# Query/key pieces moved and awaited by token span, and a new order of the side steps in a fused convolution, attention and expert kernel

## The reference, cut to what matters

```
x = x + conv(group_norm(x))      # 16 images, 192 channels, 32 x 32
t = tokens(x)                    # 1024 tokens of 192 channels per image
t = t + attention(layer_norm(t)) # 6 heads of 32, window of 33 keys around each token, plus token 0
t = t + experts(layer_norm(t))   # 4 experts (hidden 768), each token goes to the best 2

conv:  a linear recurrence with 16 states over rows and over columns, both directions,
       plus a gate g = sigmoid(W2 gelu(W1 layer_norm(x))),  result g*y + (1-g)*x
```

## Time and profile before

| | us |
|---|---|
| median of 3 runs | 3558.24 |
| lowest, highest | 3534.18, 3563.71 |
| the profiled execution's own time | 3556.88 |
| its span, first to last instruction | 3555.1 |
| PE busy | 2775.2 (78% of the span) |
| DVE busy | 1944.4 (55%) |
| ACT busy | 1040.5 (29%) |
| POOL busy | 916.0 (26%) |
| granted PE clock, mean | 0.754 of full |

### The profile page before, as it was taken

How to read it: one execution, slowest core, us unless ns; L and a number is a source line. 1 busy time by engine, 2 the same in 40 slices (tenths; PEclk the granted TensorE clock), 3 DMA queues, 4 the chain that set the end, 5 groups by cost and what they waited for, 6 DMA issues and landing times. The chain is left out here.

```text
span 3555.1 us, 51690 instructions
## 1 busy us (share of the span) xinstructions
PE 2775.2 (78%) x18529; PEld 2241.9 (63%) x18529; DVE 1944.4 (55%) x5684; ACT 1040.5 (29%) x2533; POOL 916.0 (26%) x672
## 2 busy tenths in 40 slices
PE   0467686878887888878888787888878788878877
PEld 0356575667666766667666666766666676667545
DVE  4544454555655555555555555565555556555645
ACT  0031413232332424242331423232142323314222
POOL 0001212050503314050411405041230505023344
PEclk9756676786868687786868778686867869676989
DMA  4330304151332515141242514134151514324375
GB/s 44 110 97 13 82 18 114 32 138 20 94 88 59 119 55 128 32 123 35 76 101 55 128 32 129 29 84 97 50 128 32 137 21 100 82 56 112 87 173 118
DMA packets 300095, 286.96 MB, mean 81 GB/s; under 512 B 218204, under 2 KB 259390, under 8 KB 289216
## 3 DMA queue, kind: packets, MB, share of 16 engines
q1 hardware_dynamic: 239104, 192.25, 20.7%
q0 software_dynamic: 50880, 52.59, 8.5%
q10 hardware_dynamic: 9856, 38.80, 3.6%
HBM read 133.73 MB, written 73.59 MB: 58 GB/s over the span
## 5 line engine op out<-in xcount | busy, mean ns | idle before, releaser
L1562 PE MATMUL PSUM<-XT,WB 128*128 128x512 f16 x2010 | 568.9, 419 | 26.4 <-DMA META<-slots 26.3
L834 ACT ACTIVATE HF<-PSUM,WB 128x512 f32<-128x512 f32 x402 | 275.6, 689 | 825.1 <-PE PSUM L1562 821.0
L857 ACT ACTIVATE PSPT<-PSUM,NMX 94x126 f32<-94x126 f32 x1056 | 286.1, 361 | 726.9 <-DVE NMX L1148 492.8
L1634 PE MATMUL PSUM<-VW,PSPT 126*94 126x33 f32 x2112 | 374.3, 350 | 62.1 <-DVE PSPT L1132 54.8
L1634 PEld LDWEIGHTS PSUM<-VW,PSPT 126*94 126x94 f32 x2112 | 350.6, 279 | 112.7 <-DVE PSPT L1132 112.7
L1580 PE MATMUL PSUM<-WB,HHI 128*128 128x192 f16 x1608 | 411.6, 256 | 0.2
L1094 DVE TENSOR_SCALAR HHI<-HF 128x512 f16<-128x512 f32 x402 | 175.1, 436 | 431.8 <-ACT HF L834 426.3
L1581 PE MATMUL PSUM<-WB,HHI 128*128 128x192 f16 x1608 | 410.7, 255 | 0.0
L1582 PE MATMUL PSUM<-WB,HLO 128*128 128x192 f16 x1608 | 409.9, 255 | 0.0
L728 POOL DMA_INDIRECT out_dram<-Y,META x228 | 362.5, 1590 | 147.0 <-issue 77.3
L1562 PEld LDWEIGHTS PSUM<-XT,WB 128*128 128x128 f16 x2010 | 210.6, 109 | 218.1 <-issue 65.4
(11 more groups left out here) (275 smaller groups left out, 4861.7 us busy)
## 6 DMA issues: line engine op xcount, KB each, us to landing
WB<-weights SPq DMA_DIRECT2D x67, 1600.0 KB, 7.5
QST<-QT SPq DMA_DIRECT2D x288, 64.6 KB
KST<-X SPq DMA_DIRECT2D x144, 86.6 KB
KST<-XN SPq DMA_DIRECT2D x144, 86.6 KB
XR<-in_x ACTq DMA_DIRECT2D x16, 768.0 KB, 7.1
out_dram<-X ACTq DMA_DIRECT2D x32, 384.0 KB, 3.2
weights<-WB ACTq DMA_DIRECT2D x4, 1600.0 KB, 7.0
GUP<-TGU SPq DMA_DIRECT2D x256, 8.0 KB, 1.8
```

The lines of the kernel that those rows point to most:

```text
L834: act.activation(HF[:, k % 2, :], PSUM[:, 4 + k % 2, :], ACT.Gelu, scale=1 / (X_UP * W_UP), bias=bias).then_inc(f["gelu_done"], 1)
L857: e = act.activation(PS[0:QS, n % 2, h, :], PSUM[0:QS, n % 2, h * KS:(h + 1) * KS], ACT.Exp, bias=NMX[:, b, n % 2, h:h + 1])
L1562: mm = pe.matmul(dst, WB[:, ws, w:w + 128], XT[:, xs, chunk, :], start=(n == 0), stop=(n == 4))
L1634: mm = pe.matmul(PSUM[0:QS, 2, O_COL + c:O_COL + c + VC], PT[:, n % 2, h, :], VW[:, b, c:c + VC], start=True, stop=True)
```

## The change

1. **Pieces by span.** Piece n is now of kind (query, key) n // 2 % 2, half n % 2 and span n // 4: four pieces (both halves of query and of key) finish a span. The extra query column of token 0 goes with span 0.
2. **Moves by span.** `qk_moves` waits per span for four split pieces and issues 36 copies for that span, 108 in all, each over the span's 3 or 4 blocks; each span has a semaphore of its own. PE's `attention` waits for span 0 ahead of block 0, for span 1 ahead of block 4 and for span 2 ahead of block 8.
3. **Steps by number.** `til(count, k)` yields until step k. PE: the states are projected at step 3, ahead of the output product (4) and not behind it; the recurrence (L1444) at 10 and not 12; the gate products at 15, 16, 18, 19; `turn_tokens(i, 1)` at 13 and not 9, router at 16 and not 12; the output product of `rest` at 12 and not 15, `turn_tokens(i, 0)` at 20 and not 22, router at 23 and not 25; the mixing at 27 to 34 and not 26 to 34; the transposes of the first norm at 37 and 39 and not 41 and 42; the pieces from 45 and not 47. DVE: both gated inputs at 4 and not at 5 and 6, ahead of `add_attention`; `norm_tokens` at 8 and 15, not 6 and 18; `gates` at 26, positions 38, schedule 39 (before: 27, 35, 36).
4. **First norm in halves.** Statistics, power, shift, ACT's normalization (`first_norm`) and DVE's split (`first_halves`) run for tiles 0 to 3 while tiles 4 to 7 are mixed.
5. **Orders.** `block_out(j-1)` comes behind `split` of chunk 1 of block j, ahead of that iteration's side steps, and not at chunk 2 behind them. SP: `state_moves(i+1)` ahead of `expert(i, 2)`, the last copy (`state_place`) behind it. POOL: `token_rstd(i, 0)` ahead of `conv_states(i+1)`. Banks: output product 0 to 3, router 2, prefix sums 3, with the waits that follow from it.

```diff
+        def til(count, k):
+
+            while count[0] < k:
+                count[0] += 1
+                yield
...
+        GATE_AT, MIX_AT = (15, 16, 18, 19), 27
...
+        def piece_of(n):
+
+            return n // 2 % 2, n % 2, n // 4
...
-        ROUTE_BANK = [1, 2]
+        ROUTE_BANK = [2, 2]
         X2_FREE = ["x2a_free", "x2b_free"]
-        WO_BANK = [3, 2, 2, 3]
+        WO_BANK = [0, 1, 2, 3]
...
+
+            def state_place(i):
                 sp.wait_ge(s["hs_permuted"], at("hs_permuted", i, 1))
                 sp.dma_start(XG[97:113, 0, :], HST2).then_inc(s["hs_placed"], 16)
 
             def qk_moves(i):
-                for to, halves, rows in ((QST, [QHL[:, :, 0], QHL[:, :, 1]], (0, 0, 1)), (KST, KHL, (0, 1, 0))):
-                    for oh in range(2):
-                        sp.wait_ge(s["qk_split"], at("qk_split", i, 3 * oh + (3 if to is QST else 9)))
-                        for h in range(HH):
+                for span, (b0, b1) in enumerate(SPANS):
+                    sp.wait_ge(s["qk_split"], at("qk_split", i, 4 * (span + 1)))
+                    moved = s[f"qk_moved{span}"]
+                    for to, halves, rows in ((QST, [QHL[:, :, 0], QHL[:, :, 1]], (0, 0, 1)), (KST, KHL, (0, 1, 0))):
+                        for head in range(HEADS):
+                            oh, p = head // HH, head % HH * HD
                             for g, v in enumerate(rows):
-                                sp.dma_start(to[g * HD:(g + 1) * HD, oh * HH + h, :, :],
-                                             halves[oh][h * HD:(h + 1) * HD, v, :, :]).then_inc(s["qk_moved"], 16)
+                                sp.dma_start(to[g * HD:(g + 1) * HD, head, b0:b1, :],
+                                             halves[oh][p:p + HD, v, b0:b1, :]).then_inc(moved, 16)
...
             for i in range(2, B - 1):
                 selected(i)
                 input_moves(i + 1)
+                state_moves(i + 1)
                 expert(i, 2)
-                state_moves(i + 1)
+                state_place(i + 1)
                 expert(i, 3)
                 qk_moves(i + 1)
...
             def conv_tokens(i):
-                rstd(i, TR[:], TV[:], NT, "ln1_eps", "ln1_rstd")
-                pool.wait_ge(s["ln1_rstd"], at("ln1_rstd", i, 1))
-                pool.wait_ge(s["ln1_mean"], at("ln1_mean", i, 1))
-                pool.tensor_tensor(NMR[:], NMR[:], TR[:], ALU.mult).then_inc(s["ln1_shift"], 1)
+                for k in range(2):
+                    tiles = slice(4 * k, 4 * k + 4)
+                    rstd(i, TR[:, tiles], TV[:, tiles], 4, "ln1_eps", "ln1_rstd", k + 1)
...
                 token_rstd(i, 1)
+                token_rstd(i, 0)
                 if not last(i):
                     conv_states(i + 1)
-                token_rstd(i, 0)
-                if not last(i):
                     rstd(i + 1, GTR[:], GTV[:], NT, "mixln_eps", "mixln_rstd")
...
                     act.activation(TM[:, (t % 2) * C:(t % 2 + 1) * C], PSUM[:, t % 2, 0:C], ACT.Tanh, scale=0.5
                                    ).then_inc(s["mix_tanh"], 1)
-                    yield
-                    if t == 0:
-                        yield
-                yield from empty(2)
...
+                    if t == 6:
+                        first_norm(i, 0)
+                yield from til(step_no, 36)
+                first_norm(i, 1)
...
                     if k == 2:
-                        if j:
-                            block_out(i, j - 1)
                         block_gates(i, j)
                         if isinstance(i, int) and i == B:
                             block_rows(j)
                     split(i, j, k)
+                    if k == 1 and j:
+                        block_out(i, j - 1)
                     step(side, sum(STEPS[n % len(STEPS)]))
...
                 pe.wait_ge(s["piece_act"], at("piece_act", i, PIECES_QK))
                 pe.wait_ge(s["piece_dve"], at("piece_dve", i, PIECES - PIECES_QK))
-                pe.wait_ge(s["qk_moved"], at("qk_moved", i, PER["qk_moved"]))
 
                 def scores(n):
                     b, oh = n // 2, n % 2
                     if n >= 2:
                         pe.wait_ge(s["exp_done"], at("exp_done", i, n - 1))
+                    for span in range(3):
+                        if oh == 0 and b == SPANS[span][0]:
+                            moved = f"qk_moved{span}"
+                            pe.wait_ge(s[moved], at(moved, i, PER[moved]))
...
             def tail(i):
-
+                step_no = [0]
                 pe.wait_ge(s["pT_copied"], at("pT_copied", i, 2 * NB))
                 pe.wait_ge(s["o_normed"], at("o_normed", i, NB))
                 for n in range(4):
                     turn_output(n)
-                yield
-                yield
+                yield from til(step_no, 3)
                 pe.wait_ge(s["oT_copied"], at("oT_copied", i, 4))
+                if not last(i):
+                    project_states(i + 1)
+                yield from til(step_no, 4)
                 for tp in (2, 3):
                     output(i, tp)
-                yield
+                yield from til(step_no, 13)
                 if not last(i):
-                    project_states(i + 1)
-                yield
-                yield from empty(5)
+                    pe.wait_ge(s["hs_copied"], at("hs_copied", i + 1, 1))
                 turn_tokens(i, 1)
-                yield
-                yield from empty(2)
+                yield from til(step_no, 16)
                 router(i, 1)
-                yield
```

More of the change, by code:

```diff
@@ L524, in split_qk @@
         def split_qk(dve, n):
-            for ps, plain, hi, lo in piece_parts(n)[1]:
+            for ps, plain, hi, lo in piece_parts(n)[2]:
                 last = dve.tensor_tensor(lo, plain, hi, ALU.subtract)
@@ L778, in conv @@
             def conv(i):
-                yield from empty(5 if first(i) else 13)
+                step_no = [4 if first(i) else 0]
+                yield from til(step_no, 10)
                 act.wait_ge(s["scan_done"], at("scan_done", i, 1))
@@ L1005, in conv @@
             def conv(i):
-                yield from empty(0 if first(i) else 5)
+                step_no = [4 if first(i) else 0]
+                yield from til(step_no, 4)
                 dve.wait_ge(s["tanh_done"], at("tanh_done", i, 1))
@@ L1017, in conv @@
                                          ALU.add, ALU.mult).then_inc(s["gu_ready"], 1)
-                yield
-                yield from empty(2 if first(i) else 6)
                 for tp in range(NP):
+                    yield from til(step_no, GATE_AT[tp])
                     dve.wait_ge(s["xgT_done"], at("xgT_done", i, tp + 1))
@@ L1173, in cls_shift, with first_halves @@
                                          ALU.add).then_inc(s["cls_weight"], 1)
+            def first_halves(i, k):
+                tiles = slice(4 * k, 4 * k + 4)
+                if k == 0:
+                    for half in range(2):
+                        dve.wait_ge(s[X2_FREE[half]], at(X2_FREE[half], i, 1))
+                dve.wait_ge(s["xn1_ready"], at("xn1_ready", i, k + 1))
+                link(dve.tensor_scalar(XNR[:, tiles, 0:C], XN[:, tiles, 0:C], X_UP, None, ALU.mult))
+                dve.scalar_tensor_tensor(XNR[:, tiles, C:2 * C], XN[:, tiles, 0:C], X_UP, XNR[:, tiles, 0:C],
+                                         ALU.mult, ALU.subtract).then_inc(s["xnr_ready"], 1)
             def tail(i):
+                step_no = [0]
                 for n in (1, 3):
                     evacuate_oT(dve, n, i)
-                yield
+                yield from til(step_no, 1)
                 dve.wait_ge(s["cls_exp"], at("cls_exp", i, 1))
@@ L1256, in gates @@
                 dve.wait_ge(s["route_exp"], at("route_exp", i, 0))
-                if not (isinstance(i, int) and i == B):
-                    dve.wait_ge(s["mixed"], at("mixed", i, 1))
                 link(dve.tensor_reduce(sm1, se, AX.X, ALU.add))
@@ L1327, in rest @@
             def rest(i):
-                yield from empty(9)
+                step_no = [0]
+                yield from til(step_no, 9)
                 dve.wait_ge(s["cls_spread"], at("cls_spread", i, 1))
@@ L1433, in conv @@
             def conv(i):
-                yield from empty(4 if first(i) else 12)
+                step_no = [4 if first(i) else 0]
+                yield from til(step_no, 10)
                 pe.wait_ge(s["gu_ready"], at("gu_ready", i, 2))
@@ L1447, in conv @@
                 mm.then_inc(s["scan_done"], 1)
-                yield
-                if not first(i):
-                    pe.wait_ge(s["oT_copied"], at("oT_copied", i - 1, 6))
-                    pe.wait_ge(s["cls_ready"], at("cls_ready", i - 1, 1))
                 for tp in range(NP):
+                    yield from til(step_no, GATE_AT[tp])
                     if tp >= 2:
                         pe.wait_ge(s["h1_read"], at("h1_read", i, tp - 1))
```

(26 more changed lines are left out.)

234 lines of the change are left out of this document (95 added, 139 removed).

## The result

The changed kernel takes 3558.85 us (median of 20 runs, 3550.92 to 3566.79). The kernel before, run beside it, takes 3548.84 us (median of 20, 3534.18 to 3563.71). The ratio is 1.0029, with a 95% interval of 1.0017 to 1.0041: a hair slower, and by the 1% bound of the prediction no change. Forecast was 3488, faster, in a range of 3350 to 3600. The profiled execution took 3554.75 us (span 3552.9, mean granted clock 0.758). So the two profiles show -2 us where the medians show +10, and what follows explains the -2.

The account below looks back on a forecast made before the run. The prediction took PE's waits, and the low clock behind longer ones, as the bound. Terms summed to -6.0 us a cycle, -78 in 13, +9 for image 15: -69 from 3556.9, so 3488 us, range 3350 to 3600.

Parts of the forecast that it names:

- the nought for images 0 and 1: Images 0 and 1: the added 8.8 us would meet vanishing waits of about the same size, so no net change.
- the block output's -1.5 us in a cycle: PE's wait for a block's output: shorter with output ahead of mixing, partly moved to the mixing; -1.5 us, bounds -3.7 and +2.
- The waits inside attention: PE at blocks 4 and 8 waits 4.5 and 4.3 us for copies; +8.8 us a cycle, bounds 0 and +14.0.
- recurrence: PE's wait for the recurrence's input copies: input 4.5 us earlier, PE 6 us earlier; +1.2 us, bounds -3.7 and +3.
- normalized tokens: PE's wait for the normalized tokens goes through the new POOL and SP orders; -7.1 us a cycle, bounds -7.1 and -4.
- first norm and windows: PE's wait for the first norm shrinks as half the work lies beside the mixing; -2.5 us, bounds -5.7 and +1.
- clock: Less PE work at low clock behind removed waits: -2.3 us after the tokens, -2.6 after block output or first norm.
- `selected` behind 108 copies: SP's `selected` begins some 45 us into attention, behind the moves; costed at nothing, +5 if issues are slower.
- a clock mean above 0.77: Sign expected in the profile after: PE's mean granted clock above 0.77.
- my third rival: Copies for blocks 4 and 8 keep up, issuing hidden; 141 us off in 16 attention stages, 3347 us; chance 0.12.
- the first (waits move, 3574): Tokens won, but block output, first norm and their clock give nothing; cycle +0.6, 3574 us; chance 0.20.
- the second (0.71 us or more a copy): SP issues slower in `qk_moves`, lengthening both attention waits; no gain from 0.71 us, 3683 us at 0.80; chance 0.15.

Follow-up runs that it names:

- e1_steps_only: The changed kernel with the old half-by-half pieces, the old 36 copies and one wait ahead of attention; 3383.55 us, ratio 0.9517 to the kernel before.
- e7_gates_later: e1_steps_only with DVE's gates at step 28 instead of 26; 3306.04 us, ratio 0.9297.
- e13_after_gates: The changed kernel, its 108 copies included, with DVE's gates at step 28 instead of 26; 3484.01 us, ratio 0.9792.
- e12_output_back: e1_steps_only with the block's output back at its old place, ahead of the third chunk's gates and split; 3415.92 us, ratio 0.9608.
- e8_pool_sp_order: The kernel before with two orders alone: SP's state moves ahead of the third weight load, POOL's token power ahead of its permuting copy; 3463.72 us, ratio 0.9732.
- e5_two_sets: The changed kernel with spans 1 and 2 in one set, 72 copies in all, awaited at block 4; 3481.75 us, ratio 0.9802.
- e10_last_halved: e1_steps_only with the last nine key copies each cut in two, same bytes and one wait; 3466.19 us, ratio 0.9768.
- e6_last_on_act: e1_steps_only with the last nine key copies issued by ACT ahead of the next image's load; 3336.92 us, ratio 0.9397.

## Why the prediction was wrong, point by point

The forecast was 67 us too far below (-69 against -2 between the profiles). By the table above: images 0 and 1 hold 24 of it, the 13 cycles 39, image 15 another 7, and the earlier start gives 3 back. Two steps of the sum failed: the nought for images 0 and 1, and the block output's -1.5 us in a cycle, which with the mixing came out as +0.7 and so makes 29 of the 39. The waits inside attention, 8.8 forecast and a stage longer by 10.0, add 16 more; the smaller terms partly cancel.

**Wrong: "in images 0 and 1 the added 8.8 meets waits of about the same size that go (nought)".** The attention stages of these two grew by 9.6 and 10.9 us and their expert stages didn't shrink: 121.7 and 126.3 us against 119.8 and 124.9. The waits did go there, 4.3 and 3.5 us for the tokens in image 0, but the recurrence, which now stands ahead of the turn of the tokens, took over: its wait rose from 2.2 to 9.3 us in image 0 (the longest of its line), from 3.9 to 5.8 in image 1, with 2.1 and 1.8 us behind it at a gate product (L1446), for which DVE had not yet emptied the bank. The 9.3 us are also one of the prediction's own signs of being wrong, a recurrence that idles PE for much more than 5 us; in the cycles (4.7) it did not come. e1_steps_only shows the same stages without the added copies: 118.9 and 124.5 us, so the new order is worth about one microsecond there. That the recurrence took over is read from the waits; no run moved it back. I had not read these stages and had put a cycle's pattern in their place.

**Wrong in size: the cycle, -3.0 instead of -6.0.** Term by term, with the means of images 2 to 14:

| term | forecast | measured |
|---|---|---|
| waits inside attention | +8.8 | +10.0 (the stage; the two waits are 9.7) |
| start of attention | 0 | -0.4 (8.1 to 7.7) |
| recurrence | +1.2 | +1.3 (3.5 to 4.7) |
| normalized tokens | -7.1 | -7.2 |
| block output and mixing | -1.5 | +0.7 (3.8 to 0, 0 to 4.5) |
| first norm and windows | -2.5 | -1.8 (5.0 to 2.8, 1.3 to 1.7) |
| clock | -4.9 | -5.0 |
| sum | -6.0 | -2.4; the cycle itself -3.0 |

The clock is half of the 10.0 us of work that PE no longer does at the low level (33.8 to 23.8 us of it in an expert stage). The term that failed is the block's output: the step named the mechanism (the gates still wait for POOL's 5.43 us, "the wait partly moves to the mixing") and sized it wrongly. All of it moved, and more, and e7_gates_later shows why. Before, the first tile of the mixing and a split stood ahead of the gates on DVE, and the gates waited 1.01 us for POOL (the row of L703 ends at 2344.46). DVE's rows of before, then the gates' row of after:

```profile
2341.28 0.35 DVE L1048 SCALAR_TENSOR_TENSOR X<-TM,PSUM 128x192 f32<-128x192 f32 x1
...
2344.49 0.19 DVE L1259 TENSOR_REDUCE SM<-SE 128x8 f32<-128x32 f32 x1 [1.01 <-POOL SE L703]
```

```profile
2349.12 0.19 DVE L1250 TENSOR_REDUCE SM<-SE 128x8 f32<-128x32 f32 x1 [2.99 <-POOL SE L725]
```

After, the gates are at step 26 and the mixing begins at 27: the order has turned round, the gates wait 2.99 us, and the mixing waits behind them. This misplaced step costs 75 us in the changed kernel (e13_after_gates), more than the whole forecast gain. e12_output_back shows that the moved output was worth 2.1 us in a cycle all the same.

**Off in size: the waits inside attention.** Block 4 came 22.3 to 24.0 us after block 0 and block 8 another 22.8 to 24.2, where I had put 22.7: the 36 copies of span 1 took SP from 2415.64 to 2438.91, 23.3 us or 0.65 each. Mechanism and place were right, and the price per copy was nearly so: 0.63 was closer than 0.70. In image 15 PE is faster (block 4 is reached after 16.0 us) and waits 6.8 and 6.3 us; I had taken the waits of a cycle there, which is 4 of the 7 us by which image 15 missed.

**Right.** The tokens' wait and its cause, which e8_pool_sp_order shows in a handful of lines; the recurrence in a cycle; the start wait that stays; `selected` behind 108 copies, which costs nothing (27.4 us of waits at L1540, against 26.4 in its line of before); the clock's term. The sign given for it, a clock mean above 0.77, did not come (0.758): the longer attention stages lie wholly at the low level and offset what the expert stages won. Without them, in e1_steps_only, the mean is 0.770. The rule of the Trainium skill on issuing (DMA: Bandwidth & Descriptors, "Issuing engines are not separate DMA queues"), my third rival, fails for these copies: e5_two_sets and e10_last_halved show the price per issue. What the same section says of several engines, that they save only the sequencer's time, fits e6_last_on_act in part: here that time is most of the cost, and sharing it gave half of what was forecast.

Of the rivals, the first (waits move, 3574) came nearest in time and in its mechanism for one of its two waits (the block output, not the first norm); the second (0.71 us or more a copy) did not happen.

A last point is the base. The sum was made against one execution 8 us above the median of 20. That is about a tenth of the forecast gain, but it decides between a time slightly above and slightly below the kernel before. The range was said to begin at rival 3 and began at 3350, 3 us above that rival's 3347; nothing hangs on it.

## What to carry to other kernels

Splitting a transfer so that its reader can start earlier pays only if the first part is cheaper to issue: with a price per copy, three spans of 36 copies start no earlier and add two waits. An engine's list is a queue: when a step is moved forward, look for the engine that makes its input, since a step that comes before its input holds up all that is behind it (moving it two steps later was worth 78 us). And when a loop has short first and last iterations, read those stages themselves; a gain found in the middle need not be there.

## What the runs showed of the hardware

- SBUF to SBUF copies on SP cost 0.63 to 0.71 us each to issue in most rows, whether they carried 11, 7, 4 or 3 blocks (5.66 us for nine in both kernels). The slowest nine shown here, in the kernel before beside the load of the next image, took 8.25 us, 0.92 each:

```profile
2399.43 8.25 SPq L603 DMA_DIRECT2D KST<-X  x9
```

- With ACT issuing nine of 18 such copies, the 18 took 9.5 us instead of 12.9 (e6_last_on_act and e1_steps_only, means of images 3 to 15). The two engines issued side by side for 4.6 us of that, and in this time a copy was issued every 0.4 us. Two queues are faster than one, but not twice as fast. Whether this is in the issuing or in what they issue to, no run tells.
- A wait of 3.5 us taken out of an expert stage brought a further 2 us, since PE did 4.6 us less of its work at the low level (1.2 GHz) (e7_gates_later). The clock alone can do more: in the kernel before, the expert stages of images 13 and 11 hold 30.6 and 30.0 us of idle time and took 143.9 and 152.9 us, with 20.8 and 40.8 us of work at the low level.
